# Adjacency matmuls with table as weight and 512 adjacency columns, four node blocks at a time

## The chip, the cores and the metric

One core of a Trainium2 chip runs the whole program. The metric is device time in microseconds (us), median over runs. Engines: TensorE (PE, with its weight loads PEld), VectorE (DVE), ScalarE (ACT), GpSimd (POOL) and SyncE (SP), which issues most DMAs.

## The reference

A stack of graph layers on 6250 nodes with 128 features and 106250 edges (50000 drawn ones in both directions and a self loop per node, sorted by destination). Cut to what matters here:

```python
h = relu(layernorm(x)); x = x + L0(h)   # edge MLP gives edge weights, then out[dst] += norm * (h @ W)[src]
h = relu(layernorm(x)); x = x + L1(h)   # relu(A (h W1) + b1), relu(A (. W2) + b2), A normalised adjacency
h = relu(layernorm(x)); x = x + L2(h)   # m = relu(h Wm1 + bm1) Wm2 + bm2 ; agg[dst] += m[src]
                                        # upd = relu([h, agg] Wn1 + bn1) Wn2 + bn2 ; h + upd
h = relu(layernorm(x)); x = x + L3(h)   # three convolutions out[dst] += norm * (h @ W)[src]
```

From L1 on no edge weight but the degree norms is left, so that six times the same thing is wanted: the integer matrix of edge counts (6250 x 6250) times a table of 128 features per node, with a small dense layer behind it.

## The kernel before

The program has three stages.

**Edges, twice (up to about 2040 us).** The steps of 128 edges go in groups of four through a gather (`gather`, L692) and the edge MLP, and then a second time through the weighted sum of L0. Beside it POOL fills a dense adjacency matrix `adj` in HBM (float16 counts, blocks of 128 x 128): SP writes zeros and the self loops, and POOL adds the edges with 832 indirect scatters (`scatter`, L700), in the order of the edges' destinations. A run of equal edges that goes over the end of a part of the list is kept in a "spare" block row. The scatters go on until 2776 us, long after the second edge pass.

**Dense layers (from 2040 us).** Six layers q = 0 to 5 are called gcn1, message, update, gcn3, gcn3, last. Destination nodes are 49 blocks w of 128, source nodes 49 chunks c of 128. `UNITS` is the list of work, in order: a unit (q, w, c0, c1, kind) sums `adj[w, c0:c1]` times the table over the chunks c0 to c1. Layer 0 can only take blocks whose edges have all been scattered, so it is cut into six sets of blocks (`SETS`, ends 22, 29, 36, 43, 47, 49). SP waits before a set's first piece until enough of the scatters have landed (`needed`, in batches of 32 scatters). As long as the scatters run, layer 1 is begun for the chunks whose table is there: "early" units, whose sums are kept in `acc`. The "late" units of layer 1 do the chunks that are left (42 to 48 for blocks 0 to 46). A "spare" unit heads each set and each layer, and its product is spread over the blocks by one small matmul with `slots`.

**How a unit runs.** SP loads pieces of `adj` of 14 or 21 chunks of one block (rows of 3584 or 5376 bytes per partition) into a ring of four (L633). ACT (`widen`, L878) and, from the last set on and only for whole and spare units, DVE (L1659) widen seven chunks at a time to fp32r in `wide`, a ring of six. TensorE multiplies (`add_sources`): the weight is the adjacency block `of` (128 x 128), and the moving operand is the chunk's table, first halves and rests of a split float side by side, 256 columns (L1087); for late units it is the two halves one after the other, 128 columns each, into one accumulator (L1084). So a unit's sum has destination nodes on the partitions. `add_spare` ends a unit (L1095 and L1106; L1099 and L1104 for late ones). Then the dense part of one block runs in steps that are written into the loop over pieces of work (`SUBS`), three or more subs behind the unit's end, all in program order on each engine: DVE adds the halves (`reduce_sum`, L1519), PE turns the sum (`turn_source`, L1115 to L1122), ACT copies it (`copy_source`), PE multiplies (`up`, L1133, `down`, L1142 and L1145, in float32, which are two instructions per matmul), DVE adds, normalises and splits the result into the next layer's table (`set_table`, L1604 to L1626, L1523 and L1524). The residual `x` is fetched and stored per block by POOL (64 KB, L720, L732, L734), behind all scatters in POOL's order.

```python
to = wide[:, t % SUB_RING, 0:c1 - c0, :]
of = wide[:, t % SUB_RING, c - c0, :]
last = nc.tensor.matmul(ps_sum[u % 3], of, tab[q % 2][:, c, :, :].rearrange("p t d -> p (t d)"), ...)
```

Of the kernel before, what the change touches and what calls it, by code (L numbers as in the profile page):

```python
# [4 lines left out]
P = 128  # L5
N = 6250
E = 106250
D = 128
MH = 64
HID = 256  # L10
EPS = 1e-5
# [37 lines left out]
SETS = ((0, 22), (22, 29), (29, 36), (36, 43), (43, 47), (47, 49))  # L49
# [14 lines left out]
PIECE_C = 21  # L64
AR = 4
SUB_RING = 6
LEAD = SUB_RING - 1
XR = 4
X_LAG = 2
SLOT_RING = 2  # L70
LAYERS = 6
ZERO_C = 25

EARLY = [[(0, 22, 0, 21)], [(22, 29, 0, 21), (0, 29, 21, 28)], [(29, 36, 0, 28), (0, 36, 28, 35)],
         [(36, 43, 0, 35), (0, 43, 35, 42)], [(43, 47, 0, 42)], []]
UNITS = []  # L80
for n, (w0, w1) in enumerate(SETS):
    UNITS += [(0, SPARE + n, 0, DB, "spare")] + [(0, w, 0, DB, "whole") for w in range(w0, w1)]
    UNITS += [(1, w, c0, c1, "early") for b0, b1, c0, c1 in EARLY[n] for w in range(b0, b1)]

LATE_C = {w: max((c1 for one in EARLY for b0, b1, c0, c1 in one if b0 <= w < b1), default=0) for w in range(DB)}
for q in range(1, LAYERS):
    UNITS += [(q, SPARE, 0, DB, "spare")]
    UNITS += [(q, w, LATE_C[w], DB, "late") if q == 1 and LATE_C[w] else (q, w, 0, DB, "whole") for w in range(DB)]
FIRST = {q: UNITS.index((q, SPARE, 0, DB, "spare")) for q in range(LAYERS)}
UNIT_OF = {unit[:2]: u for u, unit in enumerate(UNITS) if unit[4] in ("whole", "late")}  # L90
LAST_SET = UNITS.index((0, SPARE + EARLIER, 0, DB, "spare"))


def block_of(u):
    return UNITS[u][:2] if 0 <= u < len(UNITS) and UNITS[u][4] in ("whole", "late") else None


SUBS = []
for u, (q, w, c0, c1, kind) in enumerate(UNITS):
    late_spare = q > 1 and kind == "spare"  # L100
    ends = list(range(c0, c1, SUB)) + [c1]
    for a, b in zip(ends, ends[1:]):
        SUBS.append((u, a, b - 1 if late_spare and b == DB else b))
        if q > 1 and u == FIRST[q] + 1 and a == 2 * SUB:
            SUBS.append((u - 1, DB - 1, DB))
START, END = {}, {}
for t, (u, c0, c1) in enumerate(SUBS):
# [6 lines left out]
TURN, UP, DOWN = {}, {}, {}  # L114
for u in range(len(UNITS)):
    if block_of(u):
        e, message = END[u], UNITS[u][0] == 1
        long = u + 1 < len(UNITS) and END[u + 1] - START[u + 1] >= 4
        TURN.setdefault(min(e + (5 if message else 3) if long else e + 1, len(SUBS)), []).append(u)
        UP.setdefault(min(e + (7 if message else 5) if long else e + 2, len(SUBS)), []).append(u)  # L120
        before_late = UNITS[u][:2] == (0, DB - 1)
        DOWN.setdefault(min(e + (9 if message else 6 if before_late else 7) if long else e + 3, len(SUBS)), []).append(u)
for at in (TURN, UP, DOWN):
    assert sum((at[t] for t in sorted(at)), []) == [u for u in range(len(UNITS)) if block_of(u)]
X_USES = [(q, w) for q in (1, 2, 5) for w in range(DB)]
# [25 lines left out]
def build(nc, a, out):  # L151
# [13 lines left out]
    with ExitStack() as ctx, ExitStack() as early:  # L165
# [7 lines left out]
        place = sb("place", [P, KPAD], i32)  # L173
        needed = sb("needed", [P, EARLIER], i32)
        count16 = sb("count16", [P, KPAD], f16)
        deg = sb("deg", [P, NB, PARTS + 1])
        dinv = sb("dinv", [P, 2, NB])
        deg_ok = sb("deg_ok", [P, 2, NB])
# [4 lines left out]
        window_iota_b = sb("window_iota_b", [P, P], bf16)  # L183
# [8 lines left out]
        carry_of = deg.ap().rearrange("p b c -> p (b c)")[:, 0:DB]  # L192
# [18 lines left out]

        slots = sb("slots", [P, SLOT_RING, P], f32r)
        w_mlp_cat = sb("w_mlp_cat", [P, 2 * MH])
        w_conv = {n: sb("w_" + n, [P, D]) for n in ("L0_gnn_conv_w", "L3_gnn_W0", "L3_gnn_W1", "L3_gnn_W2")}
# [3 lines left out]
        b_row = {n: sb("b_" + n, [P, D]) for n in ("L0_gnn_conv_b", "L1_gnn_b2", "L2_gnn_bm2", "L2_gnn_bn2",  # L218
                                                   "L3_gnn_b0", "L3_gnn_b1", "L3_gnn_b2")}
        b_col = {n: sb("b_" + n, [P, 2]) for n in ("L1_gnn_b1", "L2_gnn_bm1", "L2_gnn_bn1")}  # L220
        b_mlp1 = sb("b_mlp1", [P, MH])
        w_mlp2 = sb("w_mlp2", [P, MH])
# [7 lines left out]
        src_of = sb("src_of", [P, KPAD], i32, early)  # L230
        zero16 = sb("zero16", [P, ZERO_C * P], f16, early)
# [33 lines left out]
        tanh_half = sb("tanh_half", [P, 2, S], f32, early)  # L265

# [36 lines left out]
        pieces = sb("pieces", [P, AR, PIECE_C, P], f16)  # L303
        wide = sb("wide", [P, SUB_RING, SUB, P], f32r)
        neg_ident = sb("neg_ident", [P, P], f32r)
        x_rows = sb("x_rows", [P, XR, D])
        spare_parts = sb("spare_parts", [P, HALVES, D], f32r)
        summed_f = sb("summed_f", [P, D])
        source = sb("source", [P, 2, D])
        source_t = sb("source_t", [P, 2, D])  # L310
        hidden = sb("hidden", [P, 2, D])
        table_d = sb("table_d", [P, D])
        norm_d = sb("norm_d", [P, D])
        stats_d = sb("stats_d", [P, nc.vector.BN_STATS_DIM])
        moments_d = sb("moments_d", [P, nc.vector.BN_AGGR_DIM])
        rstd_d = sb("rstd_d", [P, 1])
# [1363 lines left out]
```

## Time and profile before

| | us |
|---|---|
| median of 3 runs | 4329.33 (4325.21 to 4333.56) |
| span of the profiled execution | 4327.8 |
| PE busy, share of the span | 3337.5 (77%) |
| PEld busy | 3083.0 (71%) |
| DVE busy | 2504.4 (58%) |
| ACT busy | 2161.5 (50%) |
| POOL busy | 2349.1 (54%) |

The profile gives the span, from the first to the last instruction; of the profiled execution's time outside it there is no record. The span lies inside the range of the runs, 1.5 us under their median, so that what lies around it is taken as 1.5 us. Busy times are of engines, not of the path: a wait of an engine that nobody waits for costs nothing. A granted clock (PEclk) of 1.00 is TensorE at 2.4 GHz, 0.50 at 1.2 GHz.

### The profile page before, as it was taken

Reading aid. Unit: us, or ns where it says so; the run is one execution under the profiler, and the core shown is the slowest. Engines: PE = TensorE matmul, PEld = TensorE weight load, DVE = VectorE, ACT = ScalarE, POOL = GpSimd, SP = SyncE. Lnnn points to the kernel's source line nnn. Section 1 sums busy time; section 2 is a strip of 40 time slices with the busy share of each in tenths; the row PEclk is TensorE's granted clock in tenths of the full one; section 3 lists DMA queues with packets and bytes.
Section 4 is the critical chain, followed back from the end, with each engine's and each line's share of the span. In section 5 each row is a group of like instructions: output and inputs, shape, how many; then the busy total and the mean of one; then the engine's idle time right before and its main releaser. Section 6 shows DMA issues by size and latency. Waiting matters only on the chain.

```text
span 4327.8 us, 90427 instructions
## 1 busy us (share of the span) xinstructions
PE 3337.5 (77%) x27918; PEld 3083.0 (71%) x27918; DVE 2504.4 (58%) x11433; ACT 2161.5 (50%) x3978; POOL 2349.1 (54%) x2044
## 2 busy tenths in 40 slices
PE   4666667644454466666997649999999999999999
PEld 3555555433333365555997639999999999999999
DVE  6666666544444799997222123477666555555444
ACT  1222222211111355555997639866555666666665
POOL 3777777777777888888888888532111000000111
PEclk8555555555555699998999779999999999999999
DMA  5999996444444699995997759835666788787897
GB/s 135 305 307 310 308 312 192 108 107 103 103 106 109 163 235 233 234 233 104 234 253 172 166 92 239 226 118 158 228 228 229 236 254 255 242 258 249 266 276 228
DMA packets 620479, 899.84 MB, mean 208 GB/s; under 512 B 192074, under 2 KB 451121, under 8 KB 620016
## 3 DMA queue, kind: packets, MB, share of 16 engines
q1 hardware_dynamic: 443568, 785.26, 57.6%
q0 software_dynamic: 171904, 107.02, 15.3%
q8 instruction: 243, 3.98, 0.4%
q10 hardware_dynamic: 4544, 1.77, 0.2%
q14 instruction: 220, 1.80, 0.1%
HBM read 699.91 MB, written 193.86 MB: 207 GB/s over the span
## 4 chain that ended last, share of the span: by engine, by line
PE 44%; POOL 32%; issue 13%; DVE 7%; DMA 4%; SPq 0%; ACT 0%; POOLq 0%; DVEq 0%; ACTq 0%
PE ps L1087 29%; POOL adj L700 24%; POOL rows L692 8%; PE ps L1001 5%; DMA adj<-count,place 4%; PE ps L983 3%; DVE same L1331 2%; PE ps L1133 2%; PE ps L1084 2%; DVE pre L1367 1%; PE ps L1142 1%; DVE scaled L1371 1%; PE ps L1145 1%; PE ps L1106 1%; PE ps L1119 0%
## 5 line engine op out<-in xcount | busy, mean ns | idle before, releaser
L1087 PE MATMUL ps<-tab,wide 128*128 128x256 f32 x14616 | 1887.2, 287 | 150.9 <-DVE summed_f L1519 129.6
L1087 PEld LDWEIGHTS ps<-tab,wide 128*128 128x128 f32 x14616 | 1799.6, 192 | 157.4 <-DVE summed_f L1519 135.0
L878 ACT CAST wide<-pieces 128x896 fp32r<-128x896 f16 x1497 | 1344.9, 939 | 545.6 <-PE ps L1087 383.9
L700 POOL DMA_INDIRECT adj<-count,place x832 | 1314.8, 1580 | 256.5 <-issue 244.4
L692 POOL DMA_INDIRECT rows<-table,src_of x880 | 844.5, 960 | 313.2 <-issue 258.7
L1659 DVE CAST wide<-pieces 128x896 fp32r<-128x896 f16 x603 | 368.6, 624 | 249.7 <-PE ps L1087 247.5
L734 POOL DMA_DIRECT2D out<-x_rows x49 | 26.7, 545 | 889.6 <-DVE x_rows L1624 881.7
L1001 PE MATMUL ps<-dst_mlp,onehot_t 128*128 x2640 | 364.6, 232 | 142.2 <-DVE pre L1367 95.6
L1001 PEld LDWEIGHTS ps<-dst_mlp,onehot_t 128*128 128x128 bf16 x2640 | 274.5, 104 | 222.2 <-issue 164.4
L1331 DVE SCALAR_TENSOR_TENSOR same<-ps,key,first_weight 128x128 bf16<-128x128 f32 x832 | 284.9, 344 | 226.1 <-PE ps L983 225.3
L813 ACT ACTIVATE onehot<-plain,norm 128x128 f32<-128x128 bf16 x880 | 281.0, 390 | 226.6 <-DVE norm L1437 226.6
L780 ACT COPY onehot_t<-ps 128x512 bf16<-128x512 bf16 x220 | 128.9, 586 | 509.3 <-PE ps L992 497.5
L1631 DVE TENSOR_SCALAR slots<-window_iota_b,deg 103x128 fp32r<-103x128 bf16 x294 | 85.9, 292 | 491.6 <-PE ps L1106 483.6
L732 POOL DMA_DIRECT2D x_list<-x_rows x98 | 53.2, 543 | 485.9 <-DVE norm_d L1511 319.7
L1015 PEld LDWEIGHTS ps<-weight_parts,onehot_b 128*128 128x128 bf16 x880 | 91.5, 104 | 293.3 <-issue 270.6
L1015 PE MATMUL ps<-weight_parts,onehot_b 128*128 128x4 bf16 x880 | 132.5, 184 | 213.1 <-DVE weight_parts L1394 210.0
L992 PE MATMUL ps<-ident_b,onehot_b 128*128 128x128 bf16 x880 | 137.8, 312 | 197.9 <-DVE onehot_b L1359 197.8
L1367 DVE TENSOR_TENSOR pre<-ps,rows 128x256 f32<-128x256 f32 x220 | 92.0, 418 | 337.6 <-DMA rows<-table,src_of 333.8
L785 ACT ACTIVATE gelu<-pre 128x256 f32<-128x256 f32 x220 | 91.5, 416 | 351.3 <-DVE pre L1367 347.1
L992 PEld LDWEIGHTS ps<-ident_b,onehot_b 128*128 128x128 bf16 x880 | 102.4, 145 | 225.4 <-DVE onehot_b L1359 214.4
L1033 PE MATMUL ps<-rows,onehot 128*128 128x128 f32 x1760 | 260.9, 293 | 0.5 <-ACT onehot L813 0.4
L1024 PE MATMUL ps<-inv_parts,low_t 128*128 128x49 bf16 x2640 | 108.8, 188 | 176.7 <-DVE low_t L1423 176.3
(259 smaller groups left out, 4525.7 us busy)
## 6 DMA issues: line engine op xcount, KB each, us to landing
pieces<-adj SPq DMA_DIRECT2D x527, 448.0 KB, 4.3
pieces<-adj SPq DMA_DIRECT2D x297, 672.0 KB, 5.3
h_rows<-rows SPq DMA_DIRECT2D x220, 256.0 KB
rows<-h_rows SPq DMA_DIRECT2D x220, 256.0 KB
pieces<-adj SPq DMA_DIRECT2D x155, 224.0 KB, 2.9
onehot_list<-onehot_b SPq DMA_DIRECT2D x220, 128.0 KB, 2.7
low_row<-low_list SPq DMA_DIRECT2D x220, 128.0 KB
plain<-onehot_list SPq DMA_DIRECT2D x220, 128.0 KB
```

Of the source, the lines that this page charges most:

```text
L692: nc.gpsimd.indirect_dma_start(out=rows_0[:, g % RING, s, :], out_offset=None, in_=table[:, :], in_offset=bass.IndirectOffsetOnAxis(ap=src ...
L700: nc.gpsimd.indirect_dma_start(out=adj[:, :], out_offset=bass.IndirectOffsetOnAxis(ap=place[:, k:k + 1], axis=0), in_=count16[:, k:k + 1], ...
L813: last = nc.scalar.activation(onehot[:, g % SUMS, s, :], plain[:, g % KEPT, s, :], ACT.Copy, scale=norm[:, g % NORMS, s:s + 1])
L878: nc.scalar.copy(to, of).then_inc(cast_act, 1)
L992: last = nc.tensor.transpose(ps_onehot_t[:, g % 2, s, :], onehot_b[:, g % HELD, s, :], ident_b[:, :])
L1001: last = nc.tensor.matmul(ps_mlp[:, g % 2, s, :], onehot_t[:, g % 2, s, :], dst_mlp[:, bass.ds(window[s], 1), part, :].rearrange("p o m -> ...
L1015: last = nc.tensor.matmul(ps_deg[:, bass.ds(window[s] * (PARTS + 1), PARTS + 1)], onehot_b[:, g % HELD, s, :], weight_parts[:, g % 2, s, : ...
L1033: last = nc.tensor.matmul(products[:, g % SUMS, s, :], onehot[:, g % SUMS, s, :], rows[:, g % RING, s, :], start=True, stop=True)
L1087: last = nc.tensor.matmul(ps_sum[u % 3], of, tab[q % 2][:, c, :, :].rearrange("p t d -> p (t d)"), start=(c == u0), stop=(kind in ("spare" ...
L1331: nc.vector.scalar_tensor_tensor(same[r % 2][:, 0:1, :], ps_key[t // KEY_BATCH % KEY_RING][:, t % KEY_BATCH:t % KEY_BATCH + 1, :], key[:, ...
L1367: nc.vector.tensor_tensor(pre[:, g % 2], ps_mlp[:, g % 2, 0:S, :], rows_0[:, g % RING, :, 0:MH], ALU.add).then_inc(e_pre, 1)
L1659: nc.vector.tensor_copy(to, of).then_inc(cast_dve, 1)
```

## The change

Blocks are taken four at a time (`GROUP`, `WIDE = 4`), 13 groups: eleven of four, one of three, one of two. The table becomes the weight, its two halves one after the other, and the moving operand is the adjacency of the group's blocks for one chunk, 512 columns. The sum comes out turned, features on the partitions, so that gcn3 and last need no transpose, and gcn1 and message get other ones (`set_aux`, `turn_sum`). The halves add up in PSUM. DVE's dense work is done on up to 512 elements per partition at once. Pieces are at most 5 chunks of four blocks (rows of 1280 or 1024 bytes, four per partition), and a piece is widened in two subs (3 and 2 chunks); DVE takes the subs of 2 chunks of all whole units, from layer 0 on, where the scatters still run. `wide` is a ring of three. `SETS` now end at 24, 32, 40, 44, 47, 49; late units start at chunk 44. The steps of the dense part are put where a count of columns has passed since the unit's end (`at_work`).

```diff
-SETS = ((0, 22), (22, 29), (29, 36), (36, 43), (43, 47), (47, 49))
+SETS = ((0, 24), (24, 32), (32, 40), (40, 44), (44, 47), (47, 49))
-PIECE_C = 21
-SUB_RING = 6
-XR = 4
-X_LAG = 2
+WIDE = 4
+GROUP = [(w, min(w + WIDE, w1)) for w0, w1 in SETS for w in range(w0, w1, WIDE)]
+PIECE_C = 5
+PIECE_SIZE = PIECE_C * WIDE * P
+SUB_SIZE = 3 * WIDE * P
+SUB_RING = 3
+XR = 2
+EARLY = [[(0, 24, 0, 24)], [(24, 32, 0, 24), (0, 32, 24, 32)], [(32, 40, 0, 32), (0, 40, 32, 40)],
+         [(40, 44, 0, 40), (0, 44, 40, 44)], [(44, 47, 0, 44)], []]
+ORDER[1] = [GS - 1] + list(range(GS - 1))
-BY_DVE = [u >= LAST_SET and UNITS[u][4] in ("whole", "spare") and c0 // SUB in (1, 3, 5) for u, c0, c1 in SUBS]
+BY_DVE = [u > 0 and UNITS[u][4] in ("whole", "spare") and (c0 // SUB in (1, 3, 5) if UNITS[u][4] == "spare" else c1 - c0 == 2)
+          for u, c0, c1, n in SUBS]
...
+BEHIND_END = {"gcn1": (4000, 13000), "message": (28000, 36000), "update": (4000, 18000), "gcn3": (None, 4000), "last": (None, 4000)}
+    if close:                       # message units with three message units behind them
+        turn, aux, up, down = ends[0], ends[1], ends[1], ends[2]
...
-                sp.dma_start(pieces[:, n % AR, 0:c1 - c0, :].rearrange("p c j -> p (c j)"),
-                             adj_rows[w, :, c0 * P:c1 * P]).then_inc(piece_in[n % AR], 16)
+                sp.dma_start(pieces[:, n % AR, 0:(w1 - w0) * (c1 - c0) * P].rearrange("p (b x) -> p b x", b=w1 - w0),
+                             adj_rows[w0:w1, :, c0 * P:c1 * P].rearrange("b p x -> p b x")).then_inc(piece_in[n % AR], 16)
...
 add_sources:
-                        last = nc.tensor.matmul(ps_sum[u % 3], of, tab[q % 2][:, c, :, :].rearrange("p t d -> p (t d)"),
-                                                start=(c == u0), stop=(kind in ("spare", "early") and c == u1 - 1))
+                        for half in range(HALVES):
+                            last = nc.tensor.matmul(ps_sum[SUMMED[u] % 2][:, 0:b * P], tab[q % 2][:, c, half, :], of,
+                                                    start=(c == u0 and half == 0), ...)
 add_spare:
+                if kind == "update":
+                    for w in range(w0, w1):
+                        for half in range(HALVES):
+                            nc.tensor.matmul(to[:, (w - w0) * P:(w - w0 + 1) * P], tab[q % 2][:, w, half, :], neg_ident[:, :], ...)
+                for half in range(HALVES):
+                    last = nc.tensor.matmul(to[:, 0:(w1 - w0) * P], spare_parts[:, half, :], slots[:, 0:(w1 - w0) * P], ...)
+            def turn_sum(k):            # message only: transposes back, one per block
+            def set_aux(k):             # gcn1: dinv; message: source; update: acc; one transpose per block
+            def up(k):                  # 2 halves x 512 columns, float32; update: two sources
+            def down(k):                # per block, as before; gcn3 and last straight from source_t
...
 vector:
+            def take_sums(k):           # one operation: times other_t, plus acc (late), or a copy, 512 wide
+            def take_turned(k):         # message: scale, bias, relu + x, measure, normalise, four blocks
+            def take_down(k, step):     # update: steps 0 to 3, one per sub; gcn3: 0 and 1; last: 0
 scalar:
+                for k in AUX.get(t - 1, ()):
+                    copy_aux(k)
+                for k in UP.get(t - 1, ()):
+                    relu_hidden(k)
+                for k in TURN.get(t - 1, ()):
+                    take_root()
 gpsimd:
+            for s in range(S):
+                pool.wait_ge(scattered[s], 16 * SCATTERS)
+            pipeline(len(X_USES), [(0, load_x), (1, store_x)])     # 256 KB each
```

## Rows read from the trace of the kernel before

**Rows 1.** Windows: stretch, length, busy time (instructions) of PE, PEld, DVE, ACT, POOL, PEclk, DMA share, GB/s.

```profile
2040.00:2259.00 219.00, 218.49 (x1814) 218.00 (x1815) 51.99 (x161) 211.84 (x299) 182.21 (x117) 0.99 0.97 245
...
2421.00:2603.00 182.00, 114.19 (x912) 112.05 (x912) 45.46 (x128) 108.98 (x142) 151.72 (x97) 0.81 0.69 152
2603.00:2736.00 133.00, 126.49 (x1011) 123.88 (x1011) 51.12 (x143) 121.43 (x156) 111.29 (x71) 0.97 0.93 233
...
2819.00:2967.00 148.00, 145.65 (x1225) 140.52 (x1225) 122.82 (x498) 94.42 (x268) 48.17 (x90) 1.00 0.37 119
...
2986.00:3369.00 383.00, 382.17 (x3235) 381.59 (x3234) 248.31 (x781) 227.77 (x399) 60.36 (x96) 1.00 0.68 223
...
3687.00:4002.00 315.00, 315.00 (x2646) 315.00 (x2644) 177.38 (x447) 196.38 (x250) 0.00 (x0) 1.00 0.81 251
```

**Rows 2.** The chain that ended last, 2715 to 2760: start, length, what.

```profile
2722.63 3.86 DMA adj<-count,place
...
2732.66 15.26 PE ps L1087 x105
...
2748.04 2.52 PE ps L1087 x21
```

**Rows 3.** Timeline, gcn3: `add_spare` of two blocks, one behind the other.

```profile
3761.66 0.28 PE L1106 MATMUL ps<-spare_parts,slots 128*128 128x256 f32 x1
...
3767.97 0.28 PE L1106 MATMUL ps<-spare_parts,slots 128*128 128x256 f32 x1
```

**Rows 4.** Timeline, update: `add_spare` of two blocks, and a `down`.

```profile
3230.20 0.28 PE L1106 MATMUL ps<-spare_parts,slots 128*128 128x256 f32 x1
...
3230.32 0.61 PE L1142 MATMUL ps<-w_L_gnn_Wn,hidden 128*128 128x128 f32 x4
...
3237.86 0.28 PE L1106 MATMUL ps<-spare_parts,slots 128*128 128x256 f32 x1
```

**Rows 5.** Timeline, message: `add_spare` of two late blocks.

```profile
2869.94 0.42 PE L1104 MATMUL ps<-spare_parts,slots 128*128 128x128 f32 x2
...
2873.17 0.42 PE L1104 MATMUL ps<-spare_parts,slots 128*128 128x128 f32 x2
```

**Rows 6.** Timeline near the start: five bfloat16 matmuls of 448 moving columns.

```profile
17.95 1.11 PE L905 MATMUL ps<-acc,spare_sum 128*128 128x448 bf16 x5
```

**Rows 7.** Line L905 alone: duration ns shortest/median/longest.

```profile
L905 PE MATMUL ps<-acc,spare_sum x14: 352/522/578, 14.8 to 18.7; 128*128 128x448 bf16 x14
```

**Rows 8.** Line L956 alone, float32, 448 columns.

```profile
L956 PE MATMUL ps<-weight,spare_sum x4: 538/788/954, 91.9 to 94.9; 128*128 128x447 f32 x2, 128*128 128x448 f32 x2
```

**Rows 9.** Timeline of VectorE, 1985 to 1992: operations on four blocks.

```profile
1986.34 0.69 DVE L1466 TENSOR_TENSOR x<-x,ps 128x512 f32<-128x512 f32 x1
1987.06 0.87 DVE L1469 BATCH_NORM_STATS2 stats<-x 128x6 f32<-128x128 f32 x4
...
1990.06 1.12 DVE L1482 TENSOR_SCALAR spare_sum<-x,moments,rstd 128x128 f32<-128x128 f32 x4
```

**Rows 10.** Timeline: three widenings in a row on VectorE.

```profile
3234.49 1.70 DVE L1659 CAST wide<-pieces 128x896 fp32r<-128x896 f16 x3
```

**Rows 11.** Timeline: seven widenings in a row on ScalarE.

```profile
2731.18 5.98 ACT L878 CAST wide<-pieces 128x896 fp32r<-128x896 f16 x7 [1.58 <-DMA pieces<-adj]
```

**Rows 12.** DMA queues, 3390 to 4010: packets, MB, share of 16 engines.

```profile
q1 hardware_dynamic: 41556, 154.44, 79.7%
```

**Rows 13.** The same view, 1500 to 1800, the second edge pass.

```profile
q1 hardware_dynamic: 57287, 69.59, 78.3%
```

**Rows 14.** Timeline: a float16 copy on VectorE beside a scatter.

```profile
2038.93 1.55 POOL L700 DMA_INDIRECT adj<-count,place  x1 [0.30 <-issue]
...
2039.17 0.63 DVE L1538 COPY spare_sum<-pieces 128x1792 f16<-128x1792 f16 x1 [1.00 <-DMA pieces<-adj]
```

**Rows 15.** Timeline: a sum of two float16 tensors on VectorE beside a scatter.

```profile
2733.75 1.09 DVE L1541 TENSOR_TENSOR spare_sum<-spare_sum,pieces 128x1792 f16<-128x1792 f16 x1
2734.00 2.26 POOL L700 DMA_INDIRECT adj<-count,place  x1 [0.30 <-issue]
```

More of the change, by code:

```diff
@@ L98 @@
-SUBS = []
-for u, (q, w, c0, c1, kind) in enumerate(UNITS):
[L100 to L105, printed above, removed]
+DONE = [u for u, unit in enumerate(UNITS) if unit[4] in ("whole", "late")]
+NUMBER = {u: k for k, u in enumerate(DONE)}
+assert [UNITS[u][:2] for u in DONE] == [(q, g) for q in range(LAYERS) for g in ORDER[q]]
@@ new lines, with cut, load @@
+SUMMED = [sum(unit[4] != "spare" for unit in UNITS[:u + 1]) for u in range(len(UNITS))]
+def cut(c0, c1, most):
+    parts = -(-(c1 - c0) // most)
+    ends = [c0 + (c1 - c0) * n // parts for n in range(parts + 1)]
+    return list(zip(ends, ends[1:]))
+PIECES, SUBS = [], []
+def load(u, c0, c1):
+    spare = UNITS[u][4] == "spare"
+    if spare and UNITS[u][0] > 0:
+        SUBS.extend((u, a, b, None) for a, b in cut(c0, c1, SUB))
+        return
+    for p0, p1 in cut(c0, c1, 2 * SUB if spare else PIECE_C):
+        PIECES.append((u, p0, p1))
+        ends = [p0, p0 + SUB, p1] if spare else [p0, p0 + (p1 - p0 + 1) // 2, p1] if p1 - p0 > 3 else [p0, p1]
+        SUBS.extend((u, a, b, len(PIECES) - 1) for a, b in zip(ends, ends[1:]) if a < b)
@@ L123, with width, at_work @@
[L123 to L125 removed]
+def width(u):
+    return 1 if UNITS[u][4] == "spare" else GROUP[UNITS[u][1]][1] - GROUP[UNITS[u][1]][0]
+def at_work(u, columns):
+    t = END[u] + 1
+    while t < len(SUBS) and columns > 0:
+        columns -= (SUBS[t][2] - SUBS[t][1]) * HALVES * max(width(SUBS[t][0]), 2) * P
+        t += 1
+    return t - 1
+TURN, AUX, UP, DOWN, TAKE = {}, {}, {}, {}, {}
@@ L126 @@
+for at in (TURN, AUX, UP, DOWN, TAKE):
+    order = sum((at[t] for t in sorted(at)), [])
+    assert order == sorted(order)
+X_USES = [k for k in range(len(DONE)) if UNITS[DONE[k]][0] in (1, 2, 5)]
 BATCH_SHIFT = 5
@@ L875, in widen, with relu_hidden @@
+            def relu_hidden(k):
+                q, g, w0, w1, kind = place_of(k)
+                act.wait_ge(upped, k + 1)
+                after(act, downed, k)
+                for half in range(2):
+                    last = nc.scalar.activation(hidden[:, half, 0:(w1 - w0) * P], ps_up[:, half, 0:(w1 - w0) * P], ACT.Relu,
+                                                bias=LAYER[q]["up_b"][:, half:half + 1])
+                last.then_inc(hidden_set, 1)
             def widen(t):
@@ L1136, in down @@
[L1136 to L1146 removed]
+                pe.wait_ge(slotted, NUMBER[u] + 1)
@@ new lines, in add_spare @@
+                for half in range(HALVES):
+                    last = nc.tensor.matmul(to[:, 0:(w1 - w0) * P], spare_parts[:, half, :], slots[:, 0:(w1 - w0) * P],
+                                            start=False, stop=(half == HALVES - 1))
+                last.then_inc(merged, 1)
+            def turn_sum(k):
+                q, g, w0, w1, kind = place_of(k)
+                pe.wait_ge(reduced, SUMMED[DONE[k]])
+                after(pe, turn_taken, k - GS)
+                for b in range(w1 - w0):
+                    last = nc.tensor.transpose(ps_turn[:, b, :], source_t[:, b * P:(b + 1) * P], ident[:, :])
+                last.then_inc(turned, 1)
@@ new lines, in set_aux @@
+            def set_aux(k):
+                q, g, w0, w1, kind = place_of(k)
+                after(pe, other_set, k)
+                if kind == "message":
+                    pe.wait_ge(sourced, k - GS + 1)
+                elif kind == "update":
+                    pe.wait_ge(acc_set, ORDER[1].index(g) + 1)
+                for w in range(w0, w1):
+                    of = {"gcn1": dinv[:, 1, w:w + 1].to_broadcast([P, P]), "message": source[:, w - w0, :], "update": acc[:, w, :]}[kind]
+                    last = nc.tensor.transpose(ps_aux[:, w - w0, :], of, ident[:, :])
+                last.then_inc(aux_set, 1)
```

636 lines of the change are left out of this document (343 added, 293 removed).

## The prediction

> **What bounds the kernel now.** I read first the windows, one per stage, then the chain that ended last, then the timeline of one block in each layer. The windows [rows 1] show two regimes. Until about 2600 us TensorE works only as fast as scatters release blocks: from 2421 to 2603 it is busy 114 of 182 us, with POOL never free. From 2603 on it is busy nearly always (126 of 133 us, then 382 of 383 in update, 315 of 315 in a gcn3 layer), at granted clock 1.00, and nothing else comes near: ACT 62%, DVE 56% in gcn3. The chain changes over at 2722.63, where a scatter's landing releases the piece that TensorE's run at 2732.66 needs [rows 2]; from there it is TensorE to the end at 4327.8. So a faster TensorE pays from about 2735 on, and before that only if the work left at 2735 shrinks.
>
> What a block costs TensorE is the distance between two `add_spare`: 6.31 us in gcn3 [rows 3], 7.66 in update [rows 4], 3.23 in message, late units [rows 5]. Inside it 21 adjacency matmuls of 256 columns take 2.52 us [rows 2], 0.120 each, where 256 columns at 2.4 GHz are 0.107. A 128-column float32 instruction takes (0.61-0.275)/3 = 0.112 (the last one's duration taken off, 0.275 as its modelled length) [rows 4]: more than its columns in one pass, 0.053. I read 0.11 as the price of a float32 weight load, which paces both forms.
>
> **Adjacency matmuls.** Four blocks and one chunk are now 4 x 0.120 = 0.480 us, with four loads, and become two matmuls of 512 columns with two loads. Five bfloat16 matmuls of 448 columns take 1.11 us [rows 6], the single one 0.352 [rows 7]: (1.11-0.352)/4 = 0.190, 3 ns over 448/2.4. So 512 columns take at least 0.216. If today's surplus of 0.013 stays per instruction, 0.227. The other end: if 0.120 is the columns' own price, 0.240 and no gain. A matmul of 512 hides the load of 0.11, so I take 0.218, next to the measured row. A whole group of four: 98 x 0.218 = 21.4 us.
>
> **Dense part of TensorE per group of four.** `slots`: 2 x 0.218 = 0.44. `down`: as now per block, 2 instructions of 0.112 in gcn3 (0.90 per group), 4 in the others (1.79). The transpose of gcn3 goes. `up` in float32: the shortest 448-column instruction is 538 ns [rows 8] against 352 in bfloat16 [rows 7], so a float32 pass takes twice the time per column; 512 columns are 0.43, 4 of them in gcn1 and message (1.72), 8 in update (3.44). `set_aux` and `turn_sum`: 0.45 each. The subtraction in update: 8 x 0.112 = 0.90. Sums: gcn3 and last 21.4+0.44+0.90 = 22.7 (now 25.2); update 21.4+0.44+0.90+0.45+3.44+1.79 = 28.4 (now 30.6); gcn1 25.8 (now about 28); message, late, five chunks: 2.18+0.44+0.45+0.45+1.72+1.79 = 7.0 (now 12.9).
>
> **Message, late.** Here VectorE takes over. Per group: `take_sums` 0.69; three more 512-wide operations of 0.69 [rows 9]; statistics 0.87 [rows 9], their aggregation and one small operation, about 0.55; a reciprocal 0.17; normalising 1.12 [rows 9]; `take_down` 0.69+0.4+0.69; slot 0.4. That is 7.7, and 0.5 of gaps. The root waits on ACT behind `relu_hidden`, which waits on PE's `up` of the group before: about 1 us. Period 9.3 us, over TensorE's 7.0. Against 12.9 now, 11.75 groups save 42 us. Bounds: 8.2 (the root hidden, saves 55) and 11 (POOL's fetch and store of 256 KB in a ring of two come late, saves 22).
>
> **Update and gcn3: bursts on VectorE.** Sustained load is light: 11 widenings of 1024 elements. Three of 896 take 1.70 [rows 10], so one of 1024 about 0.6 to 0.7, 7.5 us of 22.7; ACT's nine of 1536 at 0.84 per 896 [rows 11] (seven in 5.98) are 12.5. But the ring of three subs gives each widening only the 2.2 us of two subs, and DVE's stands behind dense steps in its order: `take_down` of gcn3 is 3 x 0.69 and then 0.65, 2.8 us, late by 0.6, if that sub is DVE's; in update three steps of about 2 us each. I charge 0.6 us a group in gcn3 (7 a layer with feeding) and 1.2 in update (15). Bounds: nothing, and double.
> Update: 12.25 x 2.26 = 28, less 15, saves 13. Each of gcn3, gcn3, last: 12.25 x 2.54 = 31, less 7, saves 24; three save 73 (rounding kept). The layer's spare unit stays in its old form and price.
>
> **DMA.** Bytes stay, rows shrink to 1280. Now a packet takes 0.797 x 16 x 620/41556 = 0.190 us at 3716 bytes in the mean [rows 12]; in the second edge pass 0.783 x 16 x 300/57287 = 0.066 at 1215 bytes [rows 13]. The line through both gives 0.068 at 1254. A whole group has 5120 packets: 5120 x 0.068/16 = 21.6 us, under TensorE's 22.7. A share of 0.97 has been held [rows 1], which makes 22.3: hidden, barely. SP's order and waits stay. POOL's new wait for the last scatters stands where its order already had it, behind them, and only x transfers are queued behind it, needed some 50 us later (message). One more `iota` at POOL's start, before the identity, is under 1 us by the bounds of such a row of 512 elements at one a cycle; I take 0. `slots` loses its second buffer: a slot is now made at the unit's start, one widening sub or more before `add_spare` asks for it; nothing in the long units, inside the 9.3 us in the late ones. The sum has two PSUM banks for three: the wait is for the unit before last, taken long ago.
>
> **Layer 0 and early units.** POOL's scatters end at 2776 as before. The sets of 40, 44, 47 and 49 become free at about 2538, 2657, 2717 and 2776, from their share of the 26 batches, 59.5 us each. TensorE needs, from 2542: 126 (set 40 with its early units, where ACT alone widens: 2.33 us per five chunks against 2.18), 72, 41, 20 us, which ends near 2805, and DMA at 0.93 there already [rows 1] gives some back. Before it was 2808. I count zero, with 15 us to either side. The larger work of the first set falls before TensorE's idle time. At message's end two `take_turned` of 5 us stand in front of widenings for update: 4 us lost.
>
> **Sum.** 4327.8 - 42 - 13 - 73 + 4 = 4204, and 1.5 around the span: 4205 us. The span of before lies 1.5 us under the median of its runs, so this is on their scale.
>
> **A rule against it.** A float16 copy of VectorE that writes four elements per cycle lay wholly inside a scatter instruction, which took its usual 1.55 us [rows 14]; a sum of two float16 tensors lengthened one to 2.26 [rows 15]. Widening has one source like the copy, so I charge nothing. The Trainium skill (Advanced Engine Details and Errata, section VectorE Performance Modes) says that VectorE's second SBUF port is shared with GpSimd, and that its two-port instructions and GpSimd's block each other. By that rule the widenings would count too; the one copy speaks against it, the sum for it.
>
> **Rivals.**
> Scatters slowed. Until 2776 VectorE gets 12 groups x 11 widenings and some spare ones, about 95 us, POOL being inside an instruction 83% of the time; rows 15 turn 1.09 us into 0.71 of delay. Scatters end up to 60 us later, all of it on the path: 4265.
> Columns at their own price (0.240): 98 x 0.022 x 12.25 = 26 us in each of four layers, 4310.
> Feeding a little short: packets 10% dearer (24 us a group) or bursts twice as long: 20 us for each of three layers, 4265. For it: rings are short and DMA near its limit.
> Slower than before: packets that jump between four blocks cost more than the line says. Place: the piece loads of gcn3 and last, then update. It decides where the 124 us are eaten over 3 x 12.25 groups, 3.4 us each: a group of 23.3 + 3.4 = 26.7 us, a packet of 0.083. At 0.108, a third of the way to today's 0.190, a group takes 34.6: 415 us more in three layers and 12.25 x 5.0 = 61 in update, about 4680. Against it stand the packets of rows 13, as short and at 0.066, though those DMAs read and write rows that lie side by side.
>
> **Chances.** Forecast (4160 to 4240) 0.50; scatters slowed 0.12; columns 0.07; feeding short 0.18; slower 0.10; better than 4160 (no bursts, no root wait) 0.03. The forecast alone would be 4160 to 4240. The range of 4130 to 4310 leaves out the slower case, half of the columns case and little below. About 0.2% (9 us) can be told from no change; faster 0.87, same 0.03, slower 0.10.
>
> **What would show it.** 512-column matmuls spaced 0.216 to 0.227, a gcn3 group near 23.3 us, message groups near 9.3 with VectorE busy throughout, scatter instructions still at 1.55 beside widenings, the last scatter at 2776, DMA share about 0.95 in gcn3. Wrong: gaps of PE before a matmul released by a DMA-fed widening (packets), or by VectorE (bursts), longer than 1 us a group; a last scatter after 2800; a spacing of 0.240.

## The result and the profile after

The changed kernel takes 4280.2 us (median of 4 runs, 4275.4 to 4286.0) against 4328.6 for the kernel before: ratio 0.9891, 95% interval 0.9877 to 0.9905, 48 us or 1.1% faster. The forecast was 4205, 124 us faster. The sign was right; three fifths of the gain did not come, and one stage, update, became slower where a small gain was forecast.

The windows of the kernel after, one per layer from message on (stretch, length, then busy time (instructions) of PE, PEld, DVE, ACT, POOL, PEclk, DMA share, GB/s):

```profile
2816.00:2923.00 107.00, 97.31 (x562) 78.63 (x561) 83.36 (x243) 63.80 (x91) 15.11 (x20) 0.98 0.55 162
2923.00:3345.00 422.00, 387.20 (x1870) 306.94 (x1868) 209.02 (x474) 193.88 (x183) 22.80 (x30) 1.00 0.68 204
3345.00:3658.00 313.00, 304.78 (x1461) 255.18 (x1461) 150.76 (x250) 168.49 (x125) 2.56 (x3) 0.99 0.82 251
3658.00:3966.00 308.00, 300.87 (x1453) 252.41 (x1452) 148.53 (x240) 168.90 (x124) 0.00 (x0) 1.00 0.84 257
3966.00:4267.00 301.00, 298.24 (x1449) 252.73 (x1447) 136.52 (x216) 167.28 (x121) 17.91 (x23) 1.00 0.90 278
```

Against [rows 1], TensorE no longer fills update (387 of 422 us; it was 382 of 383), while the granted clock stayed at 0.98 to 1.00. The stages from the last `add_spare` of one layer to that of the next, in us:

| stage | before | after | moved | forecast |
|---|---|---|---|---|
| to the end of layer 0 | 2808.1 | 2815.7 | +7.6 | 0 |
| message | 176.9 | 107.1 | -70 | -42 |
| update | 382.9 | 421.8 | +39 | -9 |
| gcn3, gcn3, last | 318.2, 315.4, 315.4 | 313.5, 307.6, 301.0 | -27 | -73 |

A group of four blocks, from one `add_spare` to the next in the timeline, where [rows 3 to 5] had one block. First update, then gcn3, last, and message:

```profile
3136.00 0.68 PE L1208 MATMUL ps<-slots,spare_parts 128*128 128x512 f32 x2
3167.92 0.45 PE L1208 MATMUL ps<-slots,spare_parts 128*128 128x512 f32 x1
...
3453.18 0.63 PE L1208 MATMUL ps<-slots,spare_parts 128*128 128x512 f32 x2
3477.49 0.63 PE L1208 MATMUL ps<-slots,spare_parts 128*128 128x512 f32 x2
...
4042.99 0.63 PE L1208 MATMUL ps<-slots,spare_parts 128*128 128x512 f32 x2
4066.59 0.63 PE L1208 MATMUL ps<-slots,spare_parts 128*128 128x512 f32 x2
...
2865.12 0.63 PE L1208 MATMUL ps<-slots,spare_parts 128*128 128x512 f32 x2
2872.88 0.63 PE L1208 MATMUL ps<-slots,spare_parts 128*128 128x512 f32 x2
```

Update takes 31.9 us (4 x 7.66 = 30.6 before, 29.6 forecast), gcn3 24.3 and the last layer 23.6 (25.2 before, 23.3 forecast), message mostly 7.8 to 8.3 (12.9 before, 9.3 forecast).

**What TensorE waits for.** The waits of update, then of the first gcn3 layer (engine, line, releaser: us in total, times, longest):

```profile
PEld ps L1191 <- DVE wide L1808: 36.6, 25, 2.4
PE ps L1191 <- DVE wide L1808: 26.7, 24, 2.1
...
PEld ps L1191 <- DVE wide L1808: 13.5, 14, 1.6
```

All are adjacency matmuls that a widening of VectorE holds up. VectorE's timeline in one group of update shows why (start, length, then idle time before it and its releaser):

```profile
3150.60 0.69 DVE L1755 TENSOR_TENSOR scattering<-scattering,ps 128x512 f32<-128x512 f32 x1 [2.00 <-PE ps L1259]
3151.33 0.69 DVE L1756 TENSOR_TENSOR scattering<-scattering,b_L_gnn_bn 128x512 f32<-128x512 f32 x1
3152.05 0.69 DVE L1758 TENSOR_TENSOR scattering<-scattering,acc 128x512 f32<-128x512 f32 x1
3152.78 0.87 DVE L1630 BATCH_NORM_STATS2 stats_d<-scattering 128x6 f32<-128x128 f32 x4
...
3154.18 0.69 DVE L1808 CAST wide<-pieces 128x1024 fp32r<-128x1024 f16 x1
...
3155.00 1.12 DVE L1642 TENSOR_SCALAR work<-scattering,moments_d,rstd_d 128x128 f32<-128x128 f32 x4
3156.15 0.69 DVE L1764 SCALAR_TENSOR_TENSOR work<-work,dinv 128x512 f32<-128x512 f32 x1
3156.88 0.51 DVE L1651 CAST tab<-work 128x512 fp32r<-128x512 f32 x1
3157.42 0.69 DVE L1652 TENSOR_TENSOR tab<-work,tab 128x512 fp32r<-128x512 f32 x1
3158.03 0.69 DVE L1808 CAST wide<-pieces 128x1024 fp32r<-128x1024 f16 x1
```

VectorE's widenings are every second sub, but the steps of `take_down` are issued at every sub, so two of them, 3.2 to 3.6 us, stand in front of a widening, where TensorE uses up two subs (ten matmuls of 0.227 us) in 2.27 us. The matmul that wants the last widening shown starts late:

```profile
3156.20 1.30 PE L1191 MATMUL ps<-wide,tab 128*128 128x512 f32 x5
3158.77 3.48 PE L1191 MATMUL ps<-wide,tab 128*128 128x512 f32 x14 [1.28 <-DVE wide L1808]
```

**Scatters.** They run 5.5 us ahead of before until 1988 us, and 14 behind at the end. POOL's timeline at 2056, 2068 and 2290 us:

```profile
2056.76 1.96 POOL L792 DMA_INDIRECT adj<-scattering  x1 [0.30 <-issue]
...
2068.09 1.55 POOL L792 DMA_INDIRECT adj<-scattering  x1 [0.30 <-issue]
...
2290.44 1.96 POOL L792 DMA_INDIRECT adj<-scattering  x1 [0.30 <-DMA adj<-scattering]
```

and VectorE's widenings at the same places, in its timeline:

```profile
2056.60 0.69 DVE L1808 CAST wide<-pieces 128x1024 fp32r<-128x1024 f16 x1 [1.57 <-PE ps L1191]
...
2068.52 0.68 DVE L1808 CAST wide<-pieces 128x1024 fp32r<-128x1024 f16 x1
...
2291.62 0.69 DVE L1808 CAST wide<-pieces 128x1024 fp32r<-128x1024 f16 x1 [1.57 <-PE ps L1191]
```

A widening that starts 0.16 us before a scatter instruction stretches it from 1.55 to 1.96 us; one that starts 0.43 us into it costs nothing; one that starts 1.18 us into it stretches it to 1.96 again. So the place of the start decides, and not only whether a widening is running when the scatter begins. Over all, 122 of the scatters from 2036 us on have a widening as their longest neighbour on VectorE and are 28.5 us longer in sum than 1.554 each.

### The profile page after: what moved, and what is told of

Its sections match the earlier page's. It is cut to its first block, busy times and chain, and to the rows that moved or that the text cites. A ratio compares the mean times of both kernels' runs of the same rounds, so it can differ in the third digit from the quotient of the medians.

```text
span 4273.7 us, 68717 instructions
## 1 busy us (share of the span) xinstructions
PE 3200.7 (75%) x19874; PEld 2605.3 (61%) x19874; DVE 2320.3 (54%) x9977; ACT 1849.1 (43%) x2781; POOL 2264.9 (53%) x1830
## 4 chain that ended last, share of the span: by engine, by line
POOL 35%; PE 34%; issue 14%; DVE 12%; DMA 4%; ACT 0%; SPq 0%; DVEq 0%; POOLq 0%; ACTq 0%
POOL adj L792 26%; PE ps L1191 22%; POOL rows L784 8%; PE ps L1096 5%; DMA adj<-scattering 3%; PE ps L1078 3%; DVE same L1456 2%; DVE pre L1492 1%; DVE scaled L1496 1%; DMA pieces<-adj 1%; DVE wide L1808 1%; PE ps L1264 1%; PE ps L1259 1%; PE ps L1208 1%; PE ps L1187 1%
## 5 line engine op out<-in xcount | busy, mean ns | idle before, releaser
L1191 PE MATMUL ps<-wide,tab 128*128 128x512 f32 (+2 forms) x7644 | 1723.9, 382 | 49.6 <-DVE wide L1808 42.4
L1191 PEld LDWEIGHTS ps<-wide,tab 128*128 128x128 f32 x7644 | 1372.3, 188 | 349.5 <-DVE wide L1808 63.3
L977 ACT CAST wide<-pieces 128x1536 fp32r<-128x1536 f16 (+4 forms) x878 | 1119.7, 1301 | 869.6 <-PE ps L1191 628.9
L792 POOL DMA_INDIRECT adj<-scattering x832 | 1336.8, 1607 | 254.1 <-issue 244.1
L1808 DVE CAST wide<-pieces 128x1024 fp32r<-128x1024 f16 (+3 forms) x752 | 501.2, 671 | 910.0 <-PE ps L1191 726.3
L824 POOL DMA_DIRECT2D out<-scattering x13 | 9.8, 754 | 841.1 <-DVE scattering L1773 841.1
L824 POOL DMA_DIRECT2D x_list<-scattering x26 | 21.0, 808 | 437.6 <-DVE work L1642 331.9
L1078 PE MATMUL ps<-ident,key 128*128 128x128 f32 x832 | 227.8, 429 | 12.6 <-DVE key L1442 12.6
```

Source lines behind the costliest of these rows:

```text
L792: nc.gpsimd.indirect_dma_start(out=adj[:, :], out_offset=bass.IndirectOffsetOnAxis(ap=place[:, k:k + 1], axis=0), in_=count16[:, k:k + 1], ...
L977: nc.scalar.copy(to, of).then_inc(cast_act, 1)
L1078: last = nc.tensor.transpose(ps_key[b % KEY_RING][:, i, :], key[:, t:t + 1].to_broadcast([P, P]), ident[:, :])
L1191: last = nc.tensor.matmul(ps_sum[SUMMED[u] % 2][:, 0:b * P], tab[q % 2][:, c, half, :], of, start=(c == u0 and half == 0), stop=(kind == " ...
L1808: nc.vector.tensor_copy(to, of).then_inc(cast_dve, 1)
```

## The experiments

The label is each kernel's name here. Unless said otherwise the base is the changed kernel, and each ratio is to the kernel before, run beside it on the same chip. `add_spare` rows give a layer's period as above.

**a_act: the widenings behind dense steps go to ScalarE.**

```diff
+BEHIND = {t + 1 + LEAD + late for at in (TAKE, TURN) for t in at for late in (0, 1)}
+BY_DVE = [d and not (t in BEHIND and t >= START[FIRST[2]]) for t, d in enumerate(BY_DVE)]
```

> Edit: from layer 2 on, the two widenings that VectorE would issue behind a dense step (TAKE or TURN) go to ScalarE; nothing else. In the changed kernel TensorE stands 3.1 us per group of update and 0.74 us per group of gcn3 before an L1191 matmul that a VectorE widening releases. Theory 1 (bursts: VectorE's widening stands behind dense steps in its own order): these gaps fall below 0.5 us and about 0, update's period goes from 31.9 to about 29.0, gcn3's from 24.3 to 23.6, the two stalls of 2.1 us in front of L1187 at the start of update go too; 12 x 2.9 + 24 x 0.7 + 4 = 56 us, time about 4225. Rival (feeding: the ring of three subs is too short, or DMA is late, whichever engine widens): the gaps stay, now before a ScalarE widening, and as ScalarE takes 0.97 us for a sub that took VectorE 0.69, the period of update is 32 or more, time 4280 to 4310.

Measured 4229.2 us, ratio 0.9772 (0.9758 to 0.9785). Update's period is 29.50 us, both gcn3 layers' 23.61:

```profile
3127.15 0.68 PE L1210 MATMUL ps<-slots,spare_parts 128*128 128x512 f32 x2
3156.65 0.68 PE L1210 MATMUL ps<-slots,spare_parts 128*128 128x512 f32 x2
...
3445.71 0.63 PE L1210 MATMUL ps<-slots,spare_parts 128*128 128x512 f32 x2
3469.32 0.63 PE L1210 MATMUL ps<-slots,spare_parts 128*128 128x512 f32 x2
```

So it was VectorE's order in front of a short ring that cost the time, and neither the ring nor the DMA by itself: this kernel leaves both as they were. One thing I expected of it did not come: at the start of update the two waits before L1187 went (3.7 us), but one of 3.3 us, for a widening of ScalarE, appeared before the adjacency matmul behind them, and from message's last `add_spare` to update's first it still takes 53.1 us (53.4 in the changed kernel).

**a_spread: one dense step between two widenings.**

```diff
-TAKE.setdefault(min(down + (0 if close else n), len(SUBS)), []).append((k, n))
+TAKE.setdefault(min(down + (0 if close else n * (2 if 1 < q < 5 and g < GS - 2 else 1)), len(SUBS)), []).append((k, n))
```

> Edit: the dense steps of a group in update and gcn3 are issued at every second sub instead of every one, so that one and not two stand between two VectorE widenings; the widenings stay with VectorE. Theory 1 (bursts): a step of up to 2.3 us and a widening of 0.69 against the 2.27 us that two subs last leave 0.5 us or so for each of the four steps: update's gap goes from 3.1 to 1 to 2 us a group, gcn3's from 0.74 to 0.1 (the last layer, with one step of 2.1 us, shows 0.09); 12 x 1.6 + 24 x 0.65 = 35 us, time about 4245. Rival (feeding): gaps unchanged, time 4280.

Measured 4254.7 us, ratio 0.9834 (0.9820 to 0.9847), 10 above the theory's time and 25 under the changed kernel. No work changed its engine and nothing was taken away, and gcn3 went to 23.61 us, update to 30.64: 1.3 of its 3.1 us went and the rest stays, by my reading because one step of 2.1 to 2.3 us with its widening of 0.69 is still longer than the 2.27 us of two subs.

**a_late: no widening on VectorE before the last set.**

```diff
-BY_DVE = [u > 0 and UNITS[u][4] in ("whole", "spare") and ...
+BY_DVE = [u >= LAST_SET and UNITS[u][4] in ("whole", "spare") and ...
```

> Edit: VectorE widens nothing before the last set, as in the kernel before; all else is the changed kernel. In the changed kernel 122 of 386 scatter instructions from 2036 us on overlap a VectorE widening, they are 28.5 us longer in sum than 1.554 us each, and the last scatter begins 14 us later than before although it was 5.5 us ahead at 1988 us. Theory (shared access of VectorE and GpSimd): without these widenings no scatter is longer, the last one begins at 2769 instead of 2789, and as TensorE's last two sets hang on it, layer 0 ends 8 to 15 us earlier: time about 4270. Rival 1 (the widenings only happened to lie there, the scatters wait for their DMAs): last scatter at 2789 as in the changed kernel, time 4280. Rival 2 (the scatters are faster but ScalarE alone cannot widen in step: 24.2 us for the widenings of a group plus 2.2 us of its dense work against TensorE's 25.8): last scatter 2769 and layer 0 no earlier, time 4280 to 4290.

Measured 4262.6 us, ratio 0.9848 (0.9834 to 0.9861): 18 us for taking back one part of the change, the widenings of VectorE that run beside the scatters (the expectation of the next run calls this part the second half). That is more than I expected. Layer 0 ends at 2799.6 instead of 2815.7. The last scatter, in POOL's timeline of this kernel:

```profile
2766.17 1.55 POOL L792 DMA_INDIRECT adj<-scattering  x1 [0.31 <-issue]
```

**b_before_dve: that part alone, VectorE's widenings beside the scatters, on the kernel before.**

```diff
-BY_DVE = [u >= LAST_SET and UNITS[u][4] in ("whole", "spare") and c0 // SUB in (1, 3, 5) ...
+BY_DVE = [u > 0 and UNITS[u][4] in ("whole", "spare") and c0 // SUB in (1, 3, 5) ...
```

> Edit: the kernel before, with the second half of the change alone: VectorE widens three of seven subs of whole and spare units from the first set on, not only from the last set. Theory (a widening beside a scatter lengthens it): the last scatter begins 10 to 20 us later than 2775, layer 0 ends 8 to 18 us later, time 4340 (4335 to 4347). Rival (in this kernel ScalarE's widening bounds the stages between the scatters, so that help is worth more than the scatters lose): 4310 to 4327.

Measured 4335.5 us, ratio 1.0024 (1.0015 to 1.0033): slower than before by 10 us (6 to 14). The last scatter starts at 2781.3 instead of 2774.9 and layer 0 ends at 2813.4 instead of 2808.1. The time is at the low end of my range, and the last scatter (6 us later, expected 10 to 20) and layer 0's end (5, expected 8 to 18) fell short of theirs. The widenings here are of 896 elements; 123 scatters have one as their longest neighbour on VectorE and take 1.64 us in the mean, 10 us more in sum, where the 122 of the changed kernel take 1.79. Most of these widenings start 0.6 us before a scatter or in its first 0.15 us, where the changed kernel's cost little or nothing too.

**a_bench: the matmul by itself.** Eight series of 16 behind the last group (4295.8 us in its single run, as expected):

```diff
+for i in range(n):
+    nc.tensor.matmul(ps_sum[i % banks][:, 0:columns], weights(i), moving[:, 0:columns], start=True, stop=True)
```

> The changed kernel, and behind its last group on TensorE eight series of 16 matmuls from buffers that are at rest, which measure an instruction by itself (spacing from one to the next): float32r with its own weights each, 512 columns, 256 and 128; the same with the same weights each time; with two PSUM banks in turn; float16 with 512, 256 and 128. Theory (13 ns of surplus per 32-bit instruction): float32r 0.227, 0.120, and 128 columns not under about 0.11; same weights 0.227 too; float16 0.216 and 0.110. Rival 1 (the weights' load shows through): the series with the same weights or the float16 ones, whose load is half as large, fall to 0.214 to 0.216, those with float32r stay. Rival 2 (writing one PSUM bank over and over costs it): the series with two banks is at 0.214. Whole time some 15 us over 4280.

TensorE's timeline of that kernel for 512 columns in float32r (here the second series, the same weights each time, with two matmuls of its neighbours) and in float16:

```profile
4276.15 4.24 PE L1291 MATMUL ps<-wide,tab 128*128 128x512 f32 x18
...
4287.51 3.63 PE L1291 MATMUL ps<-spare_sum 128*128 128x512 f16 x16
```

and the weight loads by their lines (shortest/median/longest ns):

```profile
L1291 PEld LDWEIGHTS ps<-wide,tab x80: 186/188/193, 4272.8 to 4287.3; 128*128 128x128 f32 x80
...
L1291 PEld LDWEIGHTS ps<-spare_sum x48: 96/98/101, 4287.5 to 4293.5; 128*128 128x128 f16 x48
```

(4.24 - 0.39)/17 = 0.227 and (3.63 - 0.39)/15 = 0.216 us. The first series, behind a pause, has 0.235 in the mean and 0.229 as its median. From start to start the others give, in us:

| columns | float32r | float16 |
|---|---|---|
| 512 | 0.227 | 0.216 |
| 256 | 0.120 | 0.109 |
| 128 | 0.108 | 0.056 |

Repeating the weights or changing the PSUM bank does not alter the 0.227. The surplus over the columns is 13 ns in the 32-bit form at 512 and at 256 columns, 3 in the 16-bit form. The rival of the PSUM bank is out. That of the load is neither shown nor out: float16 fell to 0.216, but naming the same weights spared no load (each matmul of that series has its 188 ns), so whether the 13 ns come from the longer load or from the 32-bit columns stays open. The 188 ns of a load are not its price in a stream: the float32r series of 128 columns has such a load for each matmul too, and runs at 0.108. The Trainium skill (TensorE: Matmul & The Clock Gate, section Back-to-back issue gap) gives columns at 2.4 GHz and 2.5 ns as the isolated gap: the float16 series agree, the float32r ones do not. It also names about 131 ns for 512 columns in a stream of loads and matmuls; nothing here comes under 216 ns. The same page of the Trainium skill, section Weight-path perf modes — Fast Weight Load (FWL) and DoubleRow, says that this faster load is on for 128 weights of any type but fp32. The 188 against 98 ns agree with that; that this mode is what makes the difference no run here shows.

**a_wide2: turned round, but two blocks wide.**

```diff
-WIDE = 4
+WIDE = 2
```

(with rings of five, and the dense steps' distances about halved)

> Edit: the same turned form with two blocks (256 moving columns) to a group instead of four; widening rings of five subs of 896 elements, rings of five pieces, and the dense steps' distances about halved so that they fall at the same time. It tells what turning round alone gives from what 512 columns give. Theory (a surplus of 13 ns per adjacency instruction, whatever its width): spacing of a 256-column instruction 0.120 us, two groups of gcn3 take 2 x (98 x 0.120 + 0.24 + 0.45) = 24.9 us against 24.3 in the changed kernel and 25.24 before, and the last layer 24.9 against 23.6; message, bound by VectorE's instructions, goes from 7.8 us per four blocks to about 9.5; update with shorter bursts about 30.9. Sum: 3 x 12.25 x 0.9 + 20 - 12 = about 41 us over the changed kernel, time 4320, so that the wide groups are nearly the whole gain. Rival (turning round alone, with fewer transposes, is the gain): 4280 to 4290.

Measured 4364.9 us, ratio 1.0088 (1.0072 to 1.0103): turning round without 512 columns is slower than before. The period of two blocks in the last two layers is 12.43 us (24.9 for four, as expected), but message takes 141.5 us (107.1 in the changed kernel): there VectorE's instructions for 256 elements cost 0.43 where those for 512 cost 0.69. Update takes 434 (422): its bursts did not shrink as I had expected, TensorE stands idle for 34 us as in the changed kernel, and the spacing of 0.120 comes on top. I had the direction, 45 us too few.

**b_best: both repairs.** The edits of a_act and a_late.

> Edit: both that gained alone: ScalarE takes the two widenings behind a dense step from layer 2 on (alone 4229.2 us, 51 under the changed kernel), and VectorE widens nothing before the last set (alone 4262.6, 18 under it). They lie in different stages. Theory (two causes, separate places: bursts behind 2920 us, scatters before 2790): the gains add, 4280.2 - 51.0 - 17.6 = 4212 us, last scatter at 2766, layer 0 ends at about 2800, update's period 29.5, gcn3's 23.61. Rival (one cause, too little widening capacity in sum): with ScalarE loaded in both places the gains overlap, 4225 to 4235.

Measured 4202.0 us, ratio 0.9715 (0.9702 to 0.9728), 78 us under the changed kernel; the two alone gave 51 and 18. They add and 10 us more, 3.5 of them because the kernel before, run beside them, was that much faster this time (4323.8 against 4327.3); in the profiled executions a_act ended layer 0 4.0 us later than the changed kernel, and a_late up to the end of layer 0 with a_act from there on makes 4201.8 against a span of 4200.1, so I see no third effect. That this kernel stands where I had forecast the changed one (4205) is luck: it still has the spacing of 0.227, 43 us that I had not counted, and it lacks most of the 36 us of bursts that I had.

**b_f16: no widening at all.** The table as two float16 halves; TensorE takes the float16 pieces as they come.

```diff
-        tab_0 = sb("tab_0", [P, NB, HALVES, D], f32r)
+        tab_0 = sb("tab_0", [P, NB, HALVES, D], f16)
-        wide = sb("wide", [P, SUB_RING, SUB_SIZE], f32r)
...
-                    of = wide[:, t % SUB_RING, (c - c0) * b * P:(c - c0 + 1) * b * P]
+                    of = moving[:, 0, c - p0, :] if kind == "spare" else moving[:, :, c - p0, :]
```

> Edit: the changed kernel with no widening at all: the table is kept as two float16 halves instead of two float32r ones, so TensorE takes the adjacency as float16 straight from the pieces (six of them in the ring instead of four, since the ring of widened subs is gone). The rounding of the table differs from the kernel's. It takes away both of VectorE's costs (bursts, scatters beside widenings) and tests what the 13 ns belong to that each 512-column instruction takes over 512/2.4 GHz. Theory (the surplus belongs to the 32-bit form): spacing 0.216, as the bfloat16 rows of the kernel before take 3 ns over their columns; a group of the last layer 98 x 0.216 + 1.4 = 22.6 instead of 23.61, update 28.2 instead of 31.9, gcn3 22.6 instead of 24.3; last scatter at 2766. Sum: -13 (last), -44 (two gcn3), -50 (update), -17 (scatters), -15 (gcn1 and message): about 4140. Rival 1 (the surplus belongs to every instruction with its own weights): spacing 0.227, 23.6 a group, about 4180. Rival 2 (DMA is the next bound: 5120 packets of 0.069 us are 22.1 us a group with no loss): periods 23 or more with TensorE waiting for pieces at a spacing of 0.216, 4160 to 4180.

Measured 4115.6 us, ratio 0.9512 (0.9499 to 0.9525): 208 to 213 us under the kernel before, the best of all, and 24 under my theory's time. `add_spare` in update and in the last layer:

```profile
3053.39 0.72 PE L1207 MATMUL ps<-slots,spare_parts 128*128 128x512 f32 x2
3081.18 0.72 PE L1207 MATMUL ps<-slots,spare_parts 128*128 128x512 f32 x2
...
3942.50 0.82 PE L1207 MATMUL ps<-slots,spare_parts 128*128 128x512 f32 x2
3965.03 0.82 PE L1207 MATMUL ps<-slots,spare_parts 128*128 128x512 f32 x2
```

27.8 and 22.5 us. The window of the last layer in this kernel, columns as above:

```profile
3826.00:4107.00 281.00, 281.00 (x1446) 144.56 (x1443) 40.76 (x70) 0.00 (x0) 17.25 (x23) 1.00 0.93 298
```

TensorE is busy 281 of 281 us at a DMA share of 0.93, so DMA does not bind there either.

**c_before_f16: the same for the kernel before.** Table and pieces in float16, adjacency still as weight.

```diff
-                    of = wide[:, t % SUB_RING, c - c0, :]
+                    of = spare_sum[:, c, :] if n is None else pieces[:, n % AR, c - PIECES[n][1], :]
```

> Edit: the kernel before (adjacency as weight, 256 moving columns of the table), with the table as two float16 halves and no widening, as in b_f16; the rounding of the table differs from the kernel's. The series of a_bench give 0.109 us for 256 columns in float16 and 0.216 for 512, so in this form a width of 512 saves nothing by itself: 4 x 0.109 x 49 = 21.4 us for four blocks against 98 x 0.216 = 21.2. Theory (what 512 columns bring in float32r is only the 13 ns of each second instruction, the rest of the turned form's gain is message's shorter VectorE work and fewer transposes): a block of gcn3 6.31 - 49 x 0.011 = 5.77 us, update 7.1, each of four layers 27 us shorter, layer 0 some 10 us: about 4210, the kernel b_f16 being 95 us under it, 70 of that in message. Rival (the turned form is worth nothing once no widening is needed): 4115 to 4140.

Measured 4218.9 us, ratio 0.9744 (0.9731 to 0.9758), 9 over my theory's time. A block of gcn3 takes 5.80 us, 23.2 for four, against 22.5 turned round. Float16 alone is worth 110 us to the old form; turning round is worth another 103 on top of it, 72 of them in message (175.5 us here, 103.8 in b_f16). The old form's message did not gain from float16: its period stays 3.23 us a block, 12.9 for four, while TensorE, idle for 5.5 us of it before, is now idle for 39, for the most part waiting for VectorE, which is busy for 2.8 of the 3.23:

```profile
PE ps L1120 <- DVE source L1509: 27.9, 37, 1.1
```

(waits from 2830 to 2950 us: in total, times, longest.) So VectorE holds that pace without TensorE's help, and what turning round won in message is, by my reading, VectorE's fewer and wider operations.

## Why the prediction was wrong in its size

The direction was right, the size was not: 48 us of 124. Three terms of the sum were mis-sized, and each has an experiment.

**What held.** TensorE bound the layers behind 2735 us, but for message. The dense sums, the transposes that go, and the DMA did as reckoned: its share is 0.90 in the last layer, where TensorE is idle for 3 of 301 us. VectorE set the pace in message, and better than my 9.3: eight of the last nine groups took 7.2 to 8.3, about the 8.2 that I had as the lower bound with the root hidden (VectorE stands 0.37 us for it). Over 12 groups that is some 14 us; the other half of the 28 is no gain of the whole, since dense work of message's last groups, of four or three blocks each now, falls in update's stage.

**The step that failed first: "A matmul of 512 hides the load of 0.11, so I take 0.218, next to the measured row."** The measured row [rows 6] was a 16-bit one. Today's surplus of 13 ns per float32r instruction, which I had as the upper of two near ends, stayed: 0.227. That is 98 x 0.009 = 0.9 us a group, over 12.25 groups and four layers 43 us. a_bench shows that the 13 ns belong to the 32-bit form at 512 columns as at 256, and b_f16 that they go with it: its last layer is 16 us shorter than b_best's, 98 x 0.011 x 12.25 = 13 of them by this. Whether "hides the load" was wrong, or the columns themselves cost more in this form, stays open.

**The second: bursts, "1.2 in update (15)".** I had priced one late widening a group. The steps come in pairs, twice a group: 3.1 us in ten groups and near 5 in the last two, some 41 us in all, 26 more than charged. The two gcn3 layers and the last one lost some 33 us to gaps of TensorE, summed from the timeline, 21 charged. a_act and a_spread show the cause. The rival "Feeding a little short" named "bursts twice as long", and that they were (74 us for 36). But where it had 20 us more for each of three layers, the three together took 12 more, and the 26 of update it did not have: that its 4265 lies near 4280 is luck. Its other half, dearer packets, fell: a_act removes the waits with the same DMA.

**The third: "Widening has one source like the copy, so I charge nothing."** a_late shows 16 us at layer 0's end and 18 in the whole time; b_before_dve, on the other kernel, 5 and 10. I had one copy as evidence [rows 14], and it happened to begin 0.24 us into the scatter, where a widening costs nothing either. The rival "Scatters slowed" named the mechanism; it had 60 us, as it took the ratio of the float16 sum [rows 15], 0.71 us of delay for 1.09 of VectorE's, for all its 95 us of widening, where 122 scatters became longer by 0.23 each, 28.5 us in sum. The rule of the Trainium skill that I had weighed against the copy (Advanced Engine Details and Errata, section VectorE Performance Modes: GpSimd's instructions and VectorE's two-port ones block each other) agrees with the stretched scatters, but not for every start of a widening: those in a scatter's first half microsecond delayed nothing. That the port is the reason no run shows. Without these widenings the turned form ends layer 0 at 2799.6 (a_late), 8.5 us before the old one: there I had counted nothing.

**The sum.** 43 (spacing) + 26 and 12 (bursts) + 16 (scatters) - 8.5 (layer 0) - 14 (message) = 74.5, where the span of 4273.7 lies 70 us over the 4204 I had for it. The terms are measured separately, the last three partly by my division of stages, so that a few microseconds in each stay uncertain. The rivals "Columns at their own price" and "Slower" fell: 0.227 is not 0.240, and packets cost 0.063 us at 1216 bytes in the last layer (63933 of them, 83.9% of 16 engines for 301 us), no more than the line said (0.068). The prediction read message's 12.9 us as TensorE's price alone; c_before_f16 shows that VectorE holds the old form at the same pace with TensorE partly idle.

## What to carry to other kernels

Take the price of an instruction from a row of the same operand type: between float32r and 16 bits a matmul's fixed part was 13 and 3 ns here, and that was a third of the forecast gain. Where an engine feeds TensorE through a short ring and does dense work in the same queue, sum what stands between two of its feeding instructions, not its load; gcn3's loss and two fifths of update's went away by only placing the steps apart. And before hiding a conversion, ask whether the matmul needs it: the operand was float16 already, and dropping the widening was worth more than the whole change (110 us in the old form), with a table that is rounded otherwise.

## What the runs showed of the hardware

A GpSimd scatter instruction of 1.55 us, with one VectorE widening (1024 elements, 0.69 us) beside it in the changed kernel, took, by the widening's start:

| start of the widening | cases | the scatter took, us |
|---|---|---|
| 0.42 to 0.58 us before it | 9 | 1.59 to 1.70 |
| 0.13 to 0.22 us before it | 31 | 1.90 to 1.99 |
| 0.04 us before to 0.48 us into it | 13 | 1.55 |
| 0.51 to 0.97 us into it | 20 | 1.64 to 1.75, four times 1.55 |
| 1.10 to 1.19 us into it | 12 | 1.87 to 1.96 |
| 1.40 to 1.51 us into it | 3 | 1.55 |

The widening was stretched too, to between 0.71 and 1.05 us, when it began 0.51 to 0.85 us into a scatter. A float32r matmul of 128 columns takes 0.108 to 0.111 us, twice its columns at 2.4 GHz (0.053), a float16 one 0.056.
